# Decoder block on one core: cross-attention scores made once and the probabilities turned, and more PSUM banks for the last group's experts

## The chip, the cores and the metric

The kernel runs on one core of a Trainium2 chip. The metric is device time in microseconds (us) of one execution; lower is better. The engines named below are TensorE (PE; PEld is its weight load), VectorE (DVE), ScalarE (ACT), GpSimd (POOL) and SyncE (SP).

## The reference

For 128 sequences of 64 tokens with 128 features, one pre-norm decoder block: agent attention, causal cross-attention to a context, and a mixture of experts. Cut to what the change touches:

```python
# cross-attention: 16 heads of 8 features
Q = split_heads(query @ Wq.T); K = split_heads(key @ Wk.T); V = split_heads(value @ Wv.T)
scores = einsum('bhqd,bhkd->bhqk', Q, K) / sqrt(8)
attn = softmax(scores + causal, axis=-1)          # over the keys k
out = merge_heads(einsum('bhqk,bhkd->bhqd', attn, V)) @ Wo.T
# experts: 16 routed (2 chosen per token) and 2 shared ones, computed for all tokens
h = silu(x @ We1 + be1) * (x @ We3 + be3)
y = sum over the chosen experts of weight * (h @ We2 + be2), plus the shared experts
```

The block is `x += attn(ln(x)); x += xattn(ln(x), ctx); x += ffn(ln(x))`.

## The kernel before

The 128 sequences are worked in 8 groups of 16 (1024 tokens, 8 tiles of 128). The program runs 9 **periods** `(e, g)`: the experts of group `e` are interleaved with the attention of the following group `g`. Period 0 is `(None, 0)`, attention alone; period 8 is `(7, None)`, experts alone. Each engine has its own instruction stream, written out by hand as a function `both(e, g)`; the engines meet through semaphores, and each runs its stream in order.

The experts are 18 **units** per group. For unit `k` TensorE makes H1 and H3 (three 128x512 products each, `up`), spreads the expert weight (C, `weight`) and runs the down-projection of unit `k-1` (`down_to`); ScalarE applies Silu to H1 (`silu`); VectorE multiplies by H3 and by C (`hidden`, two instructions), which frees the H3 and C banks and makes hT.

PSUM has 8 banks. H1, H3, C and the output Y have one bank each; attention has a ring of four. The list `attention_tiles` writes out in which order attention's tiles take the ring, and a tile may be written once its predecessor four places earlier has been read. `wait_free` is this wait, placed ahead of a tile's first matmul; `read` says which semaphore frees each tile.

Cross-attention of a group is done in four parts `u` of 256 tokens, four tiles of 128x512 each (4 heads by 64 keys by 2 token tiles). Before the change it goes through the scores twice:

1. Within units 12 to 15, `scores(g, u)` makes the four tiles S with tokens on the partitions, and VectorE's `maxima` takes the row maxima. Nothing else is read from S.
2. After unit 15, `split_shifts` splits the maxima into three bf16 parts, `turn_shifts` turns them, ScalarE moves them into `shiftT`.
3. After unit 16, for each `u`, `scores_T(g, u)` makes the four tiles ST with the keys on the partitions: first `pickT`/`shiftT` matmuls put mask and minus maxima into the bank, then 32 small matmuls add K times Q. ScalarE's `exp_x` takes Exp from PSUM into `PT`, `values` multiplies `PT` by V into O, VectorE's `normalise_O` divides by the sums, `turn_O` and `project` make Yx, and `add_x` adds it to the residual. Parts of the next group's front (`front_xn`, `front_M`) lie between.

Then come unit 17, the gate of the experts of group `g` and the next period. The first half of the gate (`apply_e(g, 0)`, `gate_shift`, `gate_groups`) is worked here, the second at the start of the next period; the next period's unit 1 needs it, through `turn_3(e, 1)` on TensorE.

On ScalarE a change between Silu and Exp puts an ACT_TABLE_LOAD into the stream.

"Stage" in the text below is the stretch from the start of unit 12 (in period 0: of the first scores) to the end of the last projection or down-projection of a period.

Of the kernel before, what the change touches and what calls it, by code (L numbers as in the profile page):

```python
# [6 lines left out]
def decoder_block(nc, x, ctx_in, Wqkv, Wo_a, bo, Wq, Wk, Wv, Wo_x, gate_w, gate_b,  # L7
# [53 lines left out]
    MOMENTS = [(), (0, 1, 2), (3, 4, 5), (6, 7)]  # L61

    def attention_tiles(e, g):
# [18 lines left out]
        add(g, *[f"S_{k}" for k in range(XS)], "mT")  # L82
        for u in range(UX):
            add(g, *[f"ST_{XQ * u + q}" for q in range(XQ)])
            if u:
                add(g, f"OT_{u - 1}")
                add(n, *[f"M_{k}" for k in MOMENTS[u]])
            else:
                add(n, "xnT1_0", "xnT1_1")
            add(g, f"O_{u}")  # L90
            if u:
                add(g, f"Yx_{u - 1}")
        add(g, "xnT3_0", "gate_0", f"OT_{UX - 1}", f"Yx_{UX - 1}")
# [8 lines left out]
    place = {}  # L102
    for ring, (tiles, n) in RINGS.items():
        for at, tile in enumerate(tiles):
            place[tile] = (ring, at % n, at // n, tiles[at - n] if at >= n else None)

    with ExitStack() as ctx:
# [3 lines left out]
        def sem(name):  # L111
# [153 lines left out]
        read["mT"] = (mT_ready, 1, 0)  # L265
        for n in range(XS):
            read |= {f"S_{n}": (mx_ready, XS, n), f"ST_{n}": (ex_ready, XS, n)}
# [15 lines left out]
        issued = {ring: 0 for ring in RINGS}  # L283

        def wait_free(pe, g, name):

            ring, k, use, before = place[name, g]
            assert RINGS[ring][0][issued[ring]] == (name, g), (name, g, RINGS[ring][0][issued[ring]])
            issued[ring] += 1
# [55 lines left out]
        def _(pool):  # L345
# [22 lines left out]
            nc.gpsimd.memset(mparts[:], 0.0)  # L368
            nc.gpsimd.memset(shiftT[:], 0.0)
            nc.gpsimd.memset(combs[:], 0.0)  # L370
            nc.gpsimd.memset(onehot3[:], 0.0)
            step(nc.gpsimd.memset(pickT[:], 0.0))
# [16 lines left out]
            step(nc.gpsimd.affine_select(out=shiftT[0:S].rearrange("p (b q) -> p b q", q=S),  # L389
                                         in_=shiftT[0:S].rearrange("p (b q) -> p b q", q=S), compare_op=ALU.is_ge,  # L390
                                         fill=MASKED, base=0, pattern=[[0, GB], [1, S]], channel_multiplier=-1))
            step(nc.gpsimd.affine_select(out=pickT[0:S], in_=pickT[0:S], compare_op=ALU.not_equal, fill=1.0, base=0,
                                         pattern=[[0, XH // 2], [0, 2], [-1, S]], channel_multiplier=1))
            for k in range(3):
                step(nc.gpsimd.affine_select(out=pickT[S:P], in_=pickT[S:P], compare_op=ALU.not_equal, fill=1.0,
                                             base=-XH * k, pattern=[[-2, XH // 2], [-1, 2], [0, S]],
                                             channel_multiplier=1))
# [57 lines left out]
        def _(pe):  # L455
# [179 lines left out]
            def turn_shifts(g):  # L635

                wait_free(pe, g, "mT")
                pe.wait_ge(mp_ready, g + 1)
                for t in range(T):
                    last = turn_over(ps(g, "mT")[:].bitcast(bf16)[S:P, P * t:P * t + P], mparts[:, t, :], identb[:])  # L640
                last.then_inc(fulled(g, "mT"), 1)

            def scores_T(g, u):

                names = [f"ST_{XQ * u + q}" for q in range(XQ)]
                if u == 0:
                    pe.wait_ge(mT_ready, g + 1)
                for q, name in enumerate(names):
                    wait_free(pe, g, name)
                    for j in range(2):  # L650
                        mm(ps(g, name)[:, 256 * j:256 * j + 256], pickT[:, 2 * q + j, :, :],  # L651
                           shiftT[:, 256 * u:256 * u + 256], start=(j == 0), stop=False, skip_group_check=True)
                for j in range(2):
                    for k in range(4):
                        b = 4 * u + k
                        for q, name in enumerate(names):
                            rr = slice(32 * q, 32 * q + 32)
                            c0 = 256 * j + S * k
# [148 lines left out]
            def both(e, g):  # L807
# [63 lines left out]
                for u in range(UX):  # L871
                    unit(e, 12 + u)
                    if g is not None:
                        scores(g, u)
# [616 lines left out]
```

## Time and profile before

| what | value |
|---|---|
| median of 3 runs | 1214.93 us (1214.87 to 1220.33) |
| the profiled execution | 1225.85 us, of which the span is 1224.1 us |
| mean granted TensorE clock (profiled) | 0.914 of full speed |
| TensorE busy / weight loads busy | 85% / 70% of the span |
| VectorE / ScalarE / GpSimd busy | 56% / 41% / 10% of the span |
| chain that ended last, by engine | PE 61%, DVE 21%, ACT 11% |

A granted clock of 1.0 is 2.4 GHz, 0.5 is 1.2 GHz; a stretch in between was partly at either. Busy shares are means over stages with different limits, so the text goes by stage.

### The profile page before, as it was taken

The page shows a single profiled execution, that of the slowest core. Times are in us where ns is not written, and L with a number is a line of the kernel's source. Part 1 is how long each engine was busy: PE and PEld are TensorE (multiplying, and loading weights), DVE is VectorE, ACT ScalarE, POOL GpSimd, SP SyncE. Part 2 cuts the span into 40 slices and gives each one's busy share as a digit, 9 for nine tenths or more (in the row PEclk, how much of TensorE's full clock was granted, in tenths as well). Part 3 has the DMA queues.
Part 4 walks back from the last instruction along what each step waited for, and adds up shares of the span by engine and source line. Part 5 has one row for each costly group of instructions (what it writes and reads, how often), then busy time and mean ns, then how long its engine had stood idle before and what let it go on. Part 6 is the DMA issues. An engine that isn't in the chain of part 4 may idle for free.

```text
span 1224.1 us, 26890 instructions
## 1 busy us (share of the span) xinstructions
PE 1034.5 (85%) x11548; PEld 852.1 (70%) x11629; DVE 687.6 (56%) x1985; ACT 496.5 (41%) x836; POOL 120.3 (10%) x125
## 2 busy tenths in 40 slices
PE   6767988989799887989789887988889897997687
PEld 5653877678676676768676776867776686766576
DVE  2554167662686447672676437782676527861564
ACT  4341344424534354433534354434544344332232
POOL 8100010100201011000201011000201001000100
PEclk9776689978999998999999998999999998996789
DMA  6100001000100001000100001000010000000000
GB/s 173 35 1 1 2 2 35 10 2 2 44 1 10 2 11 35 10 2 2 44 1 10 2 10 36 10 1 2 13 32 10 2 2 9 1 10 2 9 1 18
DMA packets 28409, 18.54 MB, mean 15 GB/s; under 512 B 7394, under 2 KB 26883, under 8 KB 28291
## 3 DMA queue, kind: packets, MB, share of 16 engines
q1 hardware_dynamic: 26402, 12.35, 3.8%
q0 software_dynamic: 1280, 4.20, 1.1%
q8 instruction: 92, 1.51, 0.5%
q10 hardware_dynamic: 608, 0.27, 0.1%
q14 instruction: 27, 0.21, 0.1%
HBM read 12.62 MB, written 4.19 MB: 14 GB/s over the span
## 4 chain that ended last, share of the span: by engine, by line
PE 61%; DVE 21%; ACT 11%; issue 4%; POOL 2%; POOLq 0%; DVEq 0%
PE banks L533 8%; PE banks L720 6%; PE banks L676 6%; PE banks L659 6%; PE banks L522 4%; PE banks L523 3%; PE banks L524 3%; ACT PXUT L997 3%; PE banks L651 3%; ACT KQ L962 3%; PE banks L771 2%; PE banks L629 2%; DVE sil L1264 2%; DVE mx L1316 2%; PE banks L490 2%
## 5 line engine op out<-in xcount | busy, mean ns | idle before, releaser
L941 ACT ACTIVATE sil<-banks,b 128x512 f32<-128x512 f32 x144 | 99.7, 693 | 213.2 <-PE banks L524 211.1
L1264 DVE SCALAR_TENSOR_TENSOR sil<-banks,b,sil 128x512 f32<-128x512 f32 x128 | 95.7, 748 | 142.0 <-ACT sil L941 125.7
L533 PE MATMUL banks<-w,hT 128*128 128x128 f32 x1152 | 158.2, 282 | 15.0 <-DVE hT L1271 8.6
L533 PEld LDWEIGHTS banks<-w,hT 128*128 128x128 f32 x1152 | 157.9, 200 | 14.3 <-DVE hT L1271 10.4
L1333 DVE RECIPROCAL rx<-banks 128x32 f32<-128x32 f32 x32 | 11.4, 358 | 237.1 <-PE banks L676 237.1
L997 ACT ACTIVATE PXUT<-banks 128x512 f32<-128x512 f32 x128 | 66.1, 602 | 154.0 <-PE banks L659 154.0
L1316 DVE TENSOR_REDUCE mx<-banks 128x8 f32<-128x512 f32 x128 | 79.4, 683 | 26.3 <-PE banks L629 26.3
L522 PE MATMUL banks<-xnT3l,w1h 128*128 128x512 f32 x144 | 75.5, 524 | 18.6 <-ACT sil L941 18.6
L1271 DVE TENSOR_TENSOR hT<-sil,banks 128x512 f32<-128x512 f32 x128 | 87.9, 687 | 4.4
L720 PE MATMUL banks<-pooled,A 128*128 128x128 f32 x512 | 77.2, 319 | 4.6 <-DVE pooled L1353 1.9
L676 PE MATMUL banks<-Vx,PXUT 128*64 128x18 f32 x2048 | 74.7, 223 | 7.4 <-ACT PXUT L997 7.4
L676 PEld LDWEIGHTS banks<-Vx,PXUT 128*64 128x64 f32 x2048 | 71.7, 154 | 12.6 <-ACT PXUT L997 9.3
L720 PEld LDWEIGHTS banks<-pooled,A 128*128 128x128 f32 x512 | 73.5, 231 | 9.5 <-issue 7.2
L490 PE MATMUL banks<-ident,xn 128*128 128x128 f32 x192 | 34.0, 325 | 47.0 <-DVE xn L1173 31.7
L659 PEld LDWEIGHTS banks<-KQ 32*128 32x128 f32 x2048 | 68.2, 208 | 7.9 <-issue 7.9
L659 PE MATMUL banks<-KQ 32*128 32x64 f32 x2048 | 72.8, 296 | 0.0
L934 ACT COPY KQ<-banks 128x256 f32<-128x256 f32 (+1 forms) x64 | 31.3, 489 | 96.8 <-PE banks L490 77.6
L522 PE MATMUL banks<-xnT3l,w3h 128*128 128x512 f32 x144 | 62.2, 432 | 7.2 <-DVE sil L1264 7.1
L934 ACT COPY M<-banks 128x512 f32<-128x512 f32 x80 | 46.9, 586 | 51.5 <-PE banks L720 30.6
L411 POOL TENSOR_TENSOR norm_a<-norm_a,mhalf 128x8 f32<-128x8 f32 x16 | 26.5, 1655 | 388.8 <-DVE norm_a L1142 388.8
L417 POOL TENSOR_TENSOR norm_e<-norm_e,mhalf 128x4 f32<-128x4 f32 x16 | 16.3, 1018 | 469.6 <-DVE norm_e L1142 469.6
L490 PEld LDWEIGHTS banks<-ident,xn 128*128 128x128 f32 x192 | 26.3, 167 | 51.2 <-DVE xn L1173 33.8
(204 smaller groups left out, 1979.5 us busy)
## 6 DMA issues: line engine op xcount, KB each, us to landing
xin<-in_x SPq DMA_DIRECT2D x8, 512.0 KB, 4.5
cin<-in_ctx SPq DMA_DIRECT2D x8, 512.0 KB, 5.7
out_x<-xr POOLq DMA_DIRECT2D x16, 256.0 KB, 2.8
KQ<-in_L_attn_Wqkv SPq DMA_DIRECT2D x3, 512.0 KB, 5.5
KQ<-in_L_ffn_We SPq DMA_DIRECT2D x2, 512.0 KB, 4.4
KQ<-in_L_attn_Wo SPq DMA_DIRECT2D x1, 512.0 KB, 8.2
w<-in_L_ffn_We SPq DMA_DIRECT2D x1, 512.0 KB
KQ<-in_L_ffn_ws SPq DMA_DIRECT2D x2, 64.0 KB, 4.4
```

What stands on the lines that cost most here:

```text
L490: last = turn_over(ps(g, name)[:, P * t:P * t + P], src[:, 4 * n + t, :], ident[:])
L522: mm(ps(e, name)[:], wh[:, 2 * p:2 * p + 2, :], xl, start=True, stop=False)
L533: mm(ps(e, name)[:, P * t:P * t + P], hT[:, k % 2, P * t:P * t + P], w2[:, pair[k], :], start=(n == 0 and t == 0), stop=False, skip_group_ ...
L659: last = mm(ps(g, name)[:, c0:c0 + S], Kx[rr, j, b, :], Qx[rr, S * b:S * b + S], start=False, stop=True, skip_group_check=True, tile_posit ...
L676: last = mm(ps(g, name)[64 * r:64 * r + 64, o0:o0 + w], PT[:, XQ * (u % 2) + j // 2, c0:c0 + S], Vx[:, 4 * u + k, j, :], start=True, stop= ...
L720: last = mm(ps(g, f"M_{n}")[:, P * k:P * k + P], A[:, 4 * (n % 4) + k, :], pooled[:], start=True, stop=True)
L934: cp(dst, ps(g, name)[:] if src is None else src).then_inc(ready, 1)
L941: nc.scalar.activation(sil[:, k % 2, :], ps(e, f"H1_{k}")[:], ACT.Silu, bias=b1[:, pair[k]:pair[k] + 1]).then_inc(sil_ready, 1)
L997: nc.scalar.activation(PT[:, k % (2 * XQ), :], ps(g, f"ST_{k}")[:], ACT.Exp).then_inc(ex_ready, 1)
L1264: V.scalar_tensor_tensor(sil[:, k % 2, :], ps(e, f"H3_{k}")[:], b3[:, p:p + 1], sil[:, k % 2, :], ALU.add, ALU.mult).then_inc(hid_ready, 1)
L1271: V.tensor_tensor(hT[:, k % 2, :], sil[:, k % 2, :], ps(e, f"C_{k}")[:], ALU.mult).then_inc(hT_ready, 1)
L1316: V.tensor_reduce(mx[:, 2 * u:2 * u + 2, 4 * q:4 * q + 4], sv, AX, ALU.max, negate=True).then_inc(mx_ready, 1)
```

## The change

The second set of scores, the split and turned maxima and all tiles and constants that they need are gone. S is now read twice by VectorE: `shifted` takes the row maximum of each tile and subtracts it, into an SBUF buffer `pr`; ScalarE takes Exp of `pr` in place; TensorE turns the four 128x128 blocks of each tile (`turn_probs_x`, tiles P in PSUM, named PT_k); ScalarE copies them into `PT` (`PT_moved`). `values` and what follows is as before. `PT` has four slots in place of eight.

The work is laid out in six steps, one for each of the units 12 to 17: in step `s`, TensorE turns part `s-1`, makes the scores of part `s`, runs unit `12+s`, turns O of part `s-2`, makes the values of part `s-1` and projects part `s-2`. The next group's `front_xn` goes to step 4 and all of `front_M` to step 5. VectorE's `norm_a` and `apply_a` of the next group move into steps 2 and 3.

In the last period the one-bank rings of H1, H3 and C take turns with three of attention's banks: odd places of the last group's tiles use banks 0, 1 and 2 of the ring; what attention tiles are left there use bank 3. From its unit 2 on, the last group's Silu also waits for hT of two units before.

```diff
@@ attention_tiles
-        add(g, *[f"S_{k}" for k in range(XS)], "mT")
-        for u in range(UX):
-            add(g, *[f"ST_{XQ * u + q}" for q in range(XQ)])
...
+        for step in range(UX + 2):
+            if 1 <= step <= UX:
+                add(g, *[f"PT_{XQ * (step - 1) + q}" for q in range(XQ)])
+            if step < UX:
+                add(g, *[f"S_{XQ * step + q}" for q in range(XQ)])
+            if step >= 2:
+                add(g, f"OT_{step - 2}")
+            if 1 <= step <= UX:
+                add(g, f"O_{step - 1}")
+            if step == UX:
                 add(n, "xnT1_0", "xnT1_1")
...
+            if step >= 2:
+                add(g, f"Yx_{step - 2}")
@@ places
+    LAST = GROUPS - 1
+    ALSO = {"h1": 0, "h3": 1, "c": 2}
...
+            if ring == "att" and (name, i) in attention_tiles(LAST, None):
+                slot = ("att", 3)
+            elif ring in ALSO and i == LAST and at % 2:
+                slot = ("att", ALSO[ring])
@@ TensorE
-            def scores_T(g, u):
...
+            def turn_probs_x(g, u):
+
+                for q in range(XQ):
+                    name = f"PT_{XQ * u + q}"
                     wait_free(pe, g, name)
...
+                    pe.wait_ge(pr_ready, XS * g + XQ * u + q + 1)
+                    for t in range(2):
+                        for j in range(2):
+                            src = pr[:, q, 256 * t + P * j:256 * t + P * j + P]
+                            c0 = 256 * j + P * t
+                            last = turn_over(ps(g, name)[:, c0:c0 + P], src, ident[:])
+                    last.then_inc(fulled(g, name), 1)
...
+                for step in range(UX + 2):
+                    if g is not None and 1 <= step <= UX:
+                        turn_probs_x(g, step - 1)
+                    if g is not None and step < UX:
+                        scores(g, step)
+                    unit(e, 12 + step)
...
+                    if step >= 2:
+                        turn_O(g, step - 2)
+                    if 1 <= step <= UX:
+                        values(g, step - 1)
...
+                    if step >= 2:
+                        project(g, step - 2)
@@ ScalarE
+                if e == LAST and k >= 2:
+                    act.wait_ge(hT_ready, UNITS * e + k - 1)
...
-                wait_full(act, g, f"ST_{k}")
-                nc.scalar.activation(PT[:, k % (2 * XQ), :], ps(g, f"ST_{k}")[:], ACT.Exp).then_inc(ex_ready, 1)
+                act.wait_ge(dx_ready, XS * g + k + 1)
+                p = pr[:, k % XQ, :]
+                nc.scalar.activation(p, p, ACT.Exp).then_inc(pr_ready, 1)
...
+                for step in range(UX + 2):
+                    if g is not None and 1 <= step <= UX:
+                        PT_moved(g, step - 1)
+                    if g is not None and step < UX:
+                        exp_x(g, XQ * step)
+                        exp_x(g, XQ * step + 1)
+                    if g is not None and 2 <= step < UX:
+                        O_moved(g, step - 2)
+                    if g is not None and step < UX:
+                        exp_x(g, XQ * step + 2)
+                        exp_x(g, XQ * step + 3)
+                    silu(e, 12 + step)
@@ VectorE
+            def shifted(g, u):
 
                 for q in range(XQ):
                     k = XQ * u + q
                     wait_full(dve, g, f"S_{k}")
...
+                    link(V.tensor_reduce(mx[:, q], sv, AX, ALU.max))
+                    if u:
+                        wait_full(dve, g, f"PT_{k - XQ}")
+                    V.tensor_tensor(pr[:, q, :].rearrange("p (h s) -> p h s", s=S), sv,
+                                    mx[:, q].unsqueeze(2).to_broadcast([P, HALF, S]), ALU.subtract).then_inc(dx_ready, 1)
...
+                for step in range(UX + 2):
+                    if g is not None and step < UX:
+                        shifted(g, step)
...
+                    hidden(e, 12 + step)
...
+                    if step == 2 and nxt is not None:
+                        dve.wait_ge(x_loaded, 16 * nxt + 16)
+                        norm_a(xin)
+                    if step == 3 and nxt is not None:
+                        apply_a(xin, 2 * nxt + 1)
+                    if 1 <= step <= UX:
+                        normalise_O(g, step - 1)
...
+                    if step >= 2:
+                        add_x(g, step - 2)
```

How the order of the streams moves is seen at three places. The first is TensorE in period 1, around the work of the second part of cross-attention. In the rows L651 and L659 are the scores made again, L685 is `turn_O`, L720 `front_M`, L676 `values`, L694 `project`. Before:

```order
L651 MATMUL banks0<-shiftT,pickT 128x256 [waits On_ready]
L651 MATMUL banks0<-shiftT,pickT 128x256
L659 MATMUL banks0<-KQ 128x64
...
L685 MATMUL banks0<-ident,KQ 128x128 [waits ex_ready]
L685 MATMUL banks0<-ident,KQ 128x128
L720 MATMUL banks1<-pooled,A1 128x128 [waits ex_ready,pooled_ready]
...
L676 MATMUL banks0<-Vx,PXUT 64x18 [waits ex_ready,OT_ready]
L676 MATMUL banks0<-Vx,PXUT 64x18 x31
L694 MATMUL banks1<-xwT,KQ 128x128 [waits OT_ready,M_ready]
```

Now, from `values` of part 1 in step 2 to the first rows of the scores of part 3 in step 3 (L653 is `values`, L672 `project`, L639 the turned probabilities, L615 the mask rows of the scores):

```order
L653 MATMUL banks1<-Vx,PXUT 64x18 [waits pT_ready,dx_ready]
L653 MATMUL banks1<-Vx,PXUT 64x18 x31
L672 MATMUL banks1<-xwT,KQ 128x128 [waits OT_ready,dx_ready]
L672 MATMUL banks1<-xwT,KQ 128x128
L639 MATMUL banks0<-ident,PXUT 128x128 [waits pr_ready,dx_ready]
...
L639 MATMUL banks0<-ident,PXUT 128x128 [waits pr_ready,OT_ready]
...
L639 MATMUL banks1<-ident,PXUT 128x128 [waits pr_ready,On_ready]
...
L639 MATMUL banks1<-ident,PXUT 128x128 [waits pr_ready,xattn_added]
L639 MATMUL banks1<-ident,PXUT 128x128 x3
L615 MATMUL banks0<-maskb,pick 64x512 [waits pT_ready] x2
L615 MATMUL banks1<-maskb,pick 64x512 [waits pT_ready] x2
```

The turned probabilities of one part now stand between two sets of scores, and their last two tiles wait in the ring for `normalise_O` (On_ready) and `add_x` (xattn_added) of earlier parts; the next scores wait for the copies of these tiles (pT_ready).

The second place is ScalarE in period 1. Before, from unit 12 on (L941 Silu, L997 Exp, L934 copies):

```order
L941 ACTIVATE sil<-banks2,b1 128x512 [waits h10_full] x5
L934 COPY shiftT<-banks1 64x1024 [waits att2_full]
L997 ACT_TABLE_LOAD
L997 ACTIVATE PXUT<-banks1 128x512 [waits att3_full]
L997 ACTIVATE PXUT<-banks0 128x512 [waits att0_full]
L997 ACTIVATE PXUT<-banks0 128x512 [waits att1_full]
L997 ACTIVATE PXUT<-banks1 128x512 [waits att2_full]
```

Now, steps 1 and 2 (L909 are copies, of P into PT where PXUT is written; L978 is Exp, L918 Silu):

```order
L909 COPY PXUT<-banks0 128x512 [waits att0_full]
...
L978 ACT_TABLE_LOAD
L978 ACTIVATE PXUT<-PXUT 128x512 [waits dx_ready] x4
L918 ACT_TABLE_LOAD
L918 ACTIVATE sil<-banks2,b1 128x512 [waits h10_full]
L909 COPY PXUT<-banks0 128x512 [waits att1_full,att0_full]
L909 COPY PXUT<-banks1 128x512 [waits att2_full]
L909 COPY PXUT<-banks1 128x512 [waits att3_full]
L909 COPY PXUT<-banks0 128x512 [waits att0_full]
L978 ACT_TABLE_LOAD
L978 ACTIVATE PXUT<-PXUT 128x512 [waits dx_ready] x2
```

Five Silus stood together and now each stands behind four Exps, with two table loads a step; the copies of the turned tiles stand behind the Silu.

The third place is VectorE in period 1, step 2 (L1303 and L1306 are `shifted`, L1251 and L1258 `hidden`, L1314 and L1315 `normalise_O`, L1321 `add_x`):

```order
L1306 TENSOR_TENSOR PXUT<-banks0,mx 128x512 [waits att0_full,vec_step]
L1251 SCALAR_TENSOR_TENSOR sil<-banks2,b3,sil 128x512 [waits sil_ready,h30_full]
L1258 TENSOR_TENSOR hT<-sil,banks3 128x512 [waits c0_full,hid_ready]
L1134 BN_STATS stats_a<-xin 128x6 [waits x_loaded]
L1134 BN_STATS stats_a<-xin 128x6 x7
...
L1129 SCALAR_TENSOR_TENSOR norm_a6<-norm_a3,norm_a5 128x8 [waits vec_step]
L1314 RECIPROCAL rx<-banks1 128x32 [waits att2_full]
L1315 TENSOR_TENSOR KQ<-banks1,rx 128x256 [waits vec_step]
L1321 TENSOR_TENSOR xr1<-xr1,banks1 128x256 [waits att3_full]
```

`normalise_O` and `add_x`, which free the banks of the first place, now stand behind `hidden`, and that waits for the Silu of the second place.

## Rows read from the trace of the kernel before

**Rows 1.** Stages by windows (length, busy us and counts per engine, PEclk): periods 0, 7; 1 to 6.

```profile
96.00:169.50 73.50, 60.10 (x854) 46.51 (x854) 22.92 (x64) 18.99 (x37) 2.28 (x2) 0.72 0.01 2
...
1080.90:1153.30 72.40, 61.43 (x883) 51.04 (x887) 27.70 (x63) 21.55 (x36) 2.30 (x2) 0.79 0.01 2
...
sum 411.41, PE 366.75 PEld 306.74 DVE 186.56 ACT 165.45 POOL 23.63; mean PE 61.13 PEld 51.12 DVE 31.09 ACT 27.58 POOL 3.94
```

**Rows 2.** Groups by line, TensorE (busy us, mean ns, idle before and its releasers).

```profile
L490 PE MATMUL banks<-ident,xn 128*128 128x128 f32 x192 | 34.0, 325 | 47.0 <-DVE xn L1173 31.7 <-DVE xn L1165 10.0 <-ACT PXUT L997 5.3
...
L659 PE MATMUL banks<-KQ 32*128 32x64 f32 x2048 | 72.8, 296 | 0.0
```

**Rows 3.** Timeline of TensorE, period 1, unit 14 and after it (start, length, count).

```profile
247.42 0.50 PE L522 MATMUL banks<-xnT3l,w1h 128*128 128x512 f32 x1
...
250.14 0.64 PE L621 MATMUL banks<-maskb,pick 32*64 32x512 bf16 x16
...
251.57 0.50 PE L522 MATMUL banks<-xnT3l,w1h 128*128 128x512 f32 x1
...
290.48 2.92 PE L720 MATMUL banks<-pooled,A 128*128 128x128 f32 x24
293.33 2.05 PE L676 MATMUL banks<-Vx,PXUT 128*64 128x18 f32 x64
...
304.68 0.60 PE L490 MATMUL banks<-ident,xn 128*128 128x128 f32 x4
```

**Rows 4.** Timeline of VectorE, periods 0 and 1.

```profile
59.69 0.69 DVE L1291 TENSOR_REDUCE m<-banks 128x64 f32<-128x512 f32 x1
60.41 0.69 DVE L1292 TENSOR_TENSOR PXUT<-banks,m 128x512 f32<-128x512 f32 x1
...
89.61 1.64 DVE L1147 BATCH_NORM_STATS2 stats_a<-xin 128x6 f32<-128x128 f32 x8
...
116.20 2.13 DVE L1165 TENSOR_SCALAR xn<-xin,norm_a 128x128 f32<-128x128 f32 x8
130.38 0.36 DVE L1333 RECIPROCAL rx<-banks 128x32 f32<-128x32 f32 x1 [12.04 <-PE banks L676]
130.77 0.42 DVE L1334 TENSOR_TENSOR KQ<-banks,rx 128x256 f32<-128x256 f32 x1
...
212.25 0.75 DVE L1264 SCALAR_TENSOR_TENSOR sil<-banks,b,sil 128x512 f32<-128x512 f32 x1 [2.62 <-ACT sil L941]
213.03 0.69 DVE L1271 TENSOR_TENSOR hT<-sil,banks 128x512 f32<-128x512 f32 x1
```

**Rows 5.** Timeline of ScalarE, periods 1 and 2.

```profile
239.04 1.08 ACT L934 COPY ctxT<-banks 128x512 f32<-128x512 f32 x2
...
326.26 0.69 ACT L941 ACTIVATE sil<-banks,b 128x512 f32<-128x512 f32 x1 [0.25 <-PE banks L524]
326.96 1.28 ACT L1009 ACT_TABLE_LOAD   x1
328.26 0.63 ACT L1009 ACTIVATE e<-e 128x512 f32<-128x512 f32 x1
```

**Rows 6.** Timeline of VectorE at the start of period 2.

```profile
315.83 0.42 DVE L1340 TENSOR_TENSOR xr<-xr,banks 128x256 f32<-128x256 f32 x1
...
317.59 0.21 DVE L1224 TENSOR_REDUCE g<-gate 128x4 f32<-128x64 f32 x1
```

**Rows 7.** Stretches of the last period, by windows.

```profile
1164.20:1168.00 3.80, 3.80 (x14) 3.04 (x14) 0.00 (x0) 2.38 (x5) 1.28 (x1) 0.50 0.02 4
...
1171.00:1189.00 18.00, 16.51 (x93) 12.35 (x94) 13.73 (x43) 5.68 (x8) 0.00 (x0) 1.00 0.01 1
```

**Rows 8.** Timeline of GpSimd and VectorE in the setup.

```profile
22.31 1.16 POOL L389 TENSOR_SCALAR_AFFINE_SELECT shiftT<-shiftT 64x1024 bf16<-64x1024 bf16 x1 [0.52 <-POOL pick L387]
...
24.91 3.78 POOL L395 TENSOR_SCALAR_AFFINE_SELECT pickT<-pickT 64x1024 bf16<-64x1024 bf16 x3
...
31.03 0.17 DVE L1122 TENSOR_REDUCE plane<-planes 128x4 f32<-128x16 f32 x1 [19.01 <-POOL spread L402]
```

More of the change, by code:

```diff
@@ L81, in attention_tiles @@
         add(n, "ctxT_0", "ctxT_1")
-        add(g, *[f"S_{k}" for k in range(XS)], "mT")
-        for u in range(UX):
-            add(g, *[f"ST_{XQ * u + q}" for q in range(XQ)])
[L85 to L88, printed above, removed]
-                add(n, "xnT1_0", "xnT1_1")
[L90 to L93, printed above, removed]
+        for step in range(UX + 2):
[8 more added lines that the diff above has]
+            if step == UX:
+                add(n, "xnT1_0", "xnT1_1")
+                add(g, "xnT3_0")
+            if step > UX:
+                add(g, "gate_0")
+                add(n, *[f"M_{k}" for k in range(8)])
+            if step >= 2:
+                add(g, f"Yx_{step - 2}")
         return tiles
@@ L101, in decoder_block @@
              "y": ([(f"Y_{c}", e) for e in range(GROUPS) for c in range(CHUNKS)], 1)}
-    place = {}
+    LAST = GROUPS - 1
+    ALSO = {"h1": 0, "h3": 1, "c": 2}
+    home, turns, place = {}, {}, {}
     for ring, (tiles, n) in RINGS.items():
-        for at, tile in enumerate(tiles):
-            place[tile] = (ring, at % n, at // n, tiles[at - n] if at >= n else None)
+        for at, (name, i) in enumerate(tiles):
+            slot = (ring, at % n)
+            if ring == "att" and (name, i) in attention_tiles(LAST, None):
+                slot = ("att", 3)
+            elif ring in ALSO and i == LAST and at % 2:
+                slot = ("att", ALSO[ring])
+            line = turns.setdefault(slot, [])
+            place[name, i] = (*slot, len(line), line[-1] if line else None)
+            line.append((name, i))
     with ExitStack() as ctx:
@@ L281, in ps @@
             return bank[place[name, g][0]][place[name, g][1]]
-        issued = {ring: 0 for ring in RINGS}
+        issued = {slot: 0 for slot in turns}
         def wait_free(pe, g, name):
             ring, k, use, before = place[name, g]
-            assert RINGS[ring][0][issued[ring]] == (name, g), (name, g, RINGS[ring][0][issued[ring]])
-            issued[ring] += 1
+            assert turns[ring, k][issued[ring, k]] == (name, g), (name, g)
+            issued[ring, k] += 1
             if before is not None:
@@ L388, in _ @@
                                                  base=32 * a, pattern=[[-1, S]], channel_multiplier=1))
[L389 to L397, printed above, removed]
             for k in range(3):
@@ L683, in turn_O @@
                 wait_free(pe, g, f"OT_{u}")
+                pe.wait_ge(On_ready, UX * g + u + 1)
                 for t in range(2):
@@ L1463, in both @@
                     gate_groups(g, 0)
-                    add_x(g, UX - 1)
-                    norm_e(g, 1)
                     gate_best(g, 0, 0)
```

169 lines of the change are left out of this document (45 added, 124 removed).

## Prediction

> **What bounds the kernel now.** I read first the page's shares (TensorE busy 85%, VectorE 56%, ScalarE 41%), then the stages by windows, then the timelines of three engines. Cross-attention with units 12 to 17 is one stage a period [rows 1]: in periods 1 to 6 six stages take 411.4 us, 68.6 each, with TensorE busy 366.75/411.41 = 89%, VectorE 45%, ScalarE 40%. So TensorE bounds this stage, and the scores made again are on its path: their small matmuls alone are 72.8 us over 8 groups [rows 2]. Periods 0 and 7 have stages of 73.5 and 72.4 us, with a mean granted clock of 0.72 and 0.79. The chain of waits says the same (61% on TensorE). The reader is to see that no engine is full after the change either; what counts is therefore whether the new waits, in order, are longer than the work they replace.
>
> **TensorE's work in the changed stage.** At a granted clock of 1.0, a unit takes 250.14 - 247.42 = 2.72, one part's scores 251.57 - 250.14 = 1.43, four transposes 0.60, one part's values 2.05, and the eight M tiles (64 records at 24 in 2.92) 7.8 [rows 3]. Four scores, six units, sixteen turned tiles, four values, M and ten short pieces (turned O, projections, turned x, gate, last down-projection), which I take at 0.6 each, make 5.7 + 16.3 + 9.6 + 8.2 + 7.8 + 6.0 = 53.6 us. If only this counted, a stage would lose 15 us. It is not what I expect to count.
>
> **The round trip of one part.** Time zero is when the four S tiles of a part are full. The added operations have near relatives in the trace: for the reduction and subtraction of a 128x512 tile from PSUM I take the soften pair, for Exp in place the agent's Exp.
>
> - VectorE: the subtraction starts 0.72 after the reduction and lasts 0.69, so four tiles take 4 x 1.41 = 5.6 [rows 4].
> - ScalarE: Exp of the last tile 0.63, to 6.3. Behind it in order stand a table load and the unit's Silu: 1.28 to 7.5, 0.69 to 8.2 [rows 5]. H1 has long been full, so the load is not hidden, unlike the one to Exp, which runs while ScalarE waits for VectorE.
> - VectorE next has `hidden` of this unit, which needs that Silu: it idles from 5.6, then 213.03 + 0.69 - 212.25 = 1.47, to 9.7. Behind it stands `normalise_O` of the part before, 0.36 + 0.42 with hand-over 0.8, to 10.5, then `add_x` 0.4, to 10.9 [rows 4].
> - TensorE: the last turned tiles may be written only when these two have freed their banks. Then four transposes 0.6, copy to PT 0.6, and the rest of the next scores 1.4, because all four of its banks were held by turned tiles: 2.6 together. Behind these waits stand, in order, the next unit and all that follows.
>
> Step by step at full clock: step 0 has no O yet, but the four copies stand behind the Silu, so 8.2 + 4 x 0.49 [rows 5] + 1.4 = 11.6. Step 1: 10.5 + 2.6 = 13.1. Step 2 has `norm_a` between `hidden` and `normalise_O`: eight statistics 1.64 [rows 4] and seven small ones 0.9 (1.76 of [rows 6] less `add_x` 0.42 and two statistics 0.4), so 10.9 + 2.6 + 2.6 = 16.1. Step 3 has `apply_a`, 2.13: 13.0, and 0.6 for the last transposes, 13.6. From there TensorE runs on: two units, values, M and ten pieces, 5.4 + 2.05 + 7.8 + 6.0 = 21.3. Ahead of step 0, the first scores wait for the copies of ctxT (to 240.12, against 239.15 for unit 12 now) and take 1.4: 2.4. The sum is 2.4 + 11.6 + 13.1 + 16.1 + 13.6 + 21.3 = 78.1 us against 68.6: 9.5 more in each of six periods. The TensorE work within the steps (unit, O, values, projection: at most 6 us from zero) ends long before 10.5, so the pauses are 4 to 6 us.
>
> **The clock.** After TensorE's pause of 9.5 us in the last period the granted clock is 0.50, that is 1.2 GHz, over the next 3.8 us of full work [rows 7]; in the stage of period 0, where TensorE and VectorE take turns, it is 0.72 on average [rows 1]. With pauses of 4 to 6 us in each step I expect the lower level behind them. If the whole of a round trip's TensorE part ran at half speed, 1.4 would be added in step 0, 2.0 in each of steps 1 and 2, 0.6 in step 3 and 2.7 in unit 16: 8.7. If none did, nothing. I take 6, nearer to the upper end, by period 0: a stage of 84.1, 15.5 more than now, 93 us over six periods.
>
> **The other terms.**
> - Period 7 has no next group: without `norm_a`, `apply_a`, M and the turned x, 78.1 - 2.6 - 2.1 - 7.8 - 1.2 = 64.4, with the clock 70.4, against 72.4: -2 (-8 to +1).
> - Period 0 has no units, so no Silu, load or `hidden`: the steps are 6.3 + 2.0 + 1.4 = 9.7, 9.8, 12.0 and 9.5, then 14.7, ahead 2.3: 58, with the clock 64, against 73.5: -9 (-15 to -7).
> - The gate's first half now comes with `add_x` and `norm_e` of the last part ahead of `result`, where VectorE waits anyway. Between them and `gate_best` it did 317.59 - 315.83 = 1.76 [rows 6] on the way to the turned xn3, for which TensorE waits 31.7 us in all [rows 2]. Eight periods: -14 (0 to -14).
> - The last group's extra banks: TensorE idles 18.00 - 16.51 = 1.5 us over six units there [rows 7] and the rest runs at its own pace, so -1 (0 to -1.5). The added wait for hT of two units before lies behind a down-projection that needs the same hT: nothing, and 0.7 a unit, one Silu, if that cover were gone.
> - Setup: GpSimd's constants of the second scores go (22.31 to 28.69 and three memsets earlier), and VectorE's first statistics wait 19 us for the end of GpSimd's list [rows 8]. I take -6, up to 6.4; nothing if TensorE's own setup ends later than that list.
> - ScalarE's 16 copies and 6 more table loads a period, and VectorE's 16 subtractions, cost only where the round trip counts them; VectorE comes to 31 + 11 of 84 us busy. No DMA is added and no queue of SP changes.
>
> Sum: 93 - 2 - 9 - 14 - 1 - 6 = +61. Against the profiled execution, 1225.85, that is 1287; the median of the runs is 0.9% under it, so **1275 us**, 5% slower. Half a per cent (6 us) is about what a measurement of this kernel can tell from no change.
>
> The Trainium skill, "ScalarE: Activation LUTs", What ACT_TABLE_LOAD costs, puts a switch at 1283 ns for the load plus some 1380 ns of drain. Here Silu ends at 326.95, the load starts at 326.96 and Exp follows at 328.26 [rows 5]: the load agrees, the drain is not there. With the drain four exposed switches a stage would add 4 x 1.38 x 7 = 39 us to the sum.
>
> **Rivals.**
> - *TensorE-bound after all (not slower).* The units fill the waits, a stage takes 53.6 + 2.4 = 56 and period 7 about 43: 6 x -12.6, -29, -25 (period 0) and -21 for starts, last group and setup, 1225.85 - 151 or 1065 in median. For it: no engine is full. Against it: the ring wait of the last turned tiles and the Silu's place are in the order, not in a budget. It decides where the four steps together fall below 50 us (52 if the clock stays high) instead of 54.4: then the stage costs 74 to 76 and the other gains pay for it. The Trainium skill, "Perfetto Trace Analysis", Optimization Strategy, advises interleaving regimes with different bounds, which is this rival; it also takes a repeated gap on the engine that should be full as a sign that the next tile finds no PSUM, which is the forecast.
> - *The same round trip at full clock.* 6 x 9.5 - 8 - 15 - 14 - 1 - 6 = +13: 1228. For it: TensorE has 2.7 us of dense work in each step. Against: the pauses.
> - *Half clock throughout*: 6 x 18.2 + 1 - 7 - 14 - 1 - 6 = +82, 1296.
> - *A drain at each switch*, by the Trainium skill's figure: about 1314. The trace speaks against it.
> - *The gain is swallowed and nothing is left*: the step pairs run 0.08 shorter a tile (an overlap that successive VectorE instructions show), 0.3 a step, 9 us in all, and the clock stays high: 1219.
>
> **How the numbers follow.** Round trip with a clock between (1250 to 1300): 0.58. Half clock throughout or the drain (1290 to 1320): 0.12. Full clock (1222 to 1240): 0.13. Nothing left (1209 to 1221): 0.07. TensorE-bound, fully or in part (below 1209): 0.10. The range of 8 in 10 runs from 1221 to 1308; the likeliest case alone has 1250 to 1300. Faster 0.10, same 0.07, slower 0.83.
>
> **What would show it.** In the changed profile: VectorE idle of about 2.6 us ahead of `hidden` (released by Silu) in steps 0 to 3; the third and fourth turned tiles of a part released by `normalise_O` and `add_x`; steps of 11 to 12, 13, 16 us at the least; granted clock well below 0.9 in the stages; TensorE busy below 80%; the first M tiles some 6 us earlier. The forecast is wrong if the last turned tiles are released by Exp, if the load ahead of Silu overlaps the last Exp's wait, or if steps come at TensorE's own 8 to 9 us.

## The result, and the profile after

The changed kernel takes **1278.74 us** in the median (1273.31 to 1279.36, 4 runs), the kernel before 1217.63 in the same series: 4.9% slower, ratio 1.0489 (95% interval 1.0441 to 1.0537). The forecast was 1275 us, slower.

The profiled execution of after is its fastest, 1273.31 us (span 1271.6, mean granted clock 0.907); that of before, 1225.85, lies 0.7% above its median. On the profiles the difference is therefore 47.5 us, on the medians 61. The page of after (shares of the span, then the chain that ended last):

```profile
PE 1008.0 (79%) x9691; PEld 811.7 (64%) x9773; DVE 769.5 (61%) x2081; ACT 623.0 (49%) x998; POOL 112.5 (9%) x117
...
PE 43%; DVE 34%; ACT 13%; issue 7%; POOL 2%; DVEq 0%; POOLq 0%
```

TensorE was 61% of that chain and is 43%; VectorE rose from 21% to 34%. No engine is full. The stages by windows, as in [rows 1]: period 0 and period 7, and the six mixed ones (the second row stands for them, all lie within 83.24 to 83.60).

```profile
79.89:140.50 60.61, 49.27 (x622) 40.70 (x622) 34.20 (x86) 27.23 (x51) 3.91 (x3) 0.77 0.01 1
...
365.32:448.80 83.48, 62.48 (x722) 49.26 (x727) 44.26 (x107) 44.28 (x67) 3.95 (x3) 0.86 0.00 1
...
1132.47:1201.10 68.63, 53.19 (x648) 40.59 (x655) 38.77 (x83) 38.05 (x56) 2.31 (x2) 0.88 0.01 2
```
```profile
sum 500.69, PE 374.44 PEld 295.43 DVE 265.56 ACT 265.73 POOL 23.70; mean PE 62.41 PEld 49.24 DVE 44.26 ACT 44.29 POOL 3.95
```

Six stages went from 411.41 to 500.69: TensorE's busy time in them rose by 8 us only, its idle time from 45 to 126. That is the loss. By stretches:

| stretch | before | after | difference | forecast |
|---|---|---|---|---|
| start to the first scores of period 0 | 96.0 | 79.89 | -16.1 | -6 (setup) |
| stage of period 0 | 73.50 | 60.61 | -12.9 | -9 |
| six mixed stages | 411.41 | 500.69 | +89.3 | +93 |
| stage of period 7 | 72.40 | 68.63 | -3.8 | -2 |
| last period, to the end of the span | 70.8 | 70.5 | -0.3 | -1 and its start |
| starts and middles of periods 1 to 7 (the rest) | | | -8.7 | -14, with the start of the last |

Two long waits, by line (busy us, mean ns, idle before and its releasers); the first is VectorE's, the second TensorE's:

```profile
L1251 DVE SCALAR_TENSOR_TENSOR sil<-banks,b,sil 128x512 f32<-128x512 f32 x128 | 96.0, 750 | 189.4 <-ACT sil L918 173.4
L639 PE MATMUL banks<-ident,PXUT 128*128 128x128 f32 x512 | 88.9, 325 | 122.1 <-DVE KQ L1315 105.9
```

The turned probabilities (L639) wait 105.9 us for `normalise_O` (L1315), and `hidden` (L1251) waits for the Silu. These are the two waits that the forecast named. The 173.4 us are over all 18 units: 101.9 of them are left in run 1 below, where only the four steps change, so the steps hold some 71, about 2.6 in each of 28. One round trip shows how they hang together; first VectorE in period 2 (the first reduction of steps 0 to 3, and all of step 2):

```profile
367.70 0.69 DVE L1303 TENSOR_REDUCE mx<-banks 128x8 f32<-128x512 f32 x1 [4.51 <-PE banks L623]
...
380.55 0.69 DVE L1303 TENSOR_REDUCE mx<-banks 128x8 f32<-128x512 f32 x1 [3.23 <-PE banks L623]
...
395.11 0.69 DVE L1303 TENSOR_REDUCE mx<-banks 128x8 f32<-128x512 f32 x1 [4.21 <-PE banks L623]
...
399.81 0.69 DVE L1306 TENSOR_TENSOR PXUT<-banks,mx 128x512 f32<-128x512 f32 x1
403.26 0.75 DVE L1251 SCALAR_TENSOR_TENSOR sil<-banks,b,sil 128x512 f32<-128x512 f32 x1 [2.76 <-ACT sil L918]
404.05 0.69 DVE L1258 TENSOR_TENSOR hT<-sil,banks 128x512 f32<-128x512 f32 x1
404.65 1.64 DVE L1134 BATCH_NORM_STATS2 stats_a<-xin 128x6 f32<-128x128 f32 x8
...
407.52 0.42 DVE L1315 TENSOR_TENSOR KQ<-banks,rx 128x256 f32<-128x256 f32 x1
407.86 0.41 DVE L1321 TENSOR_TENSOR xr<-xr,banks 128x256 f32<-128x256 f32 x1
...
413.15 0.69 DVE L1303 TENSOR_REDUCE mx<-banks 128x8 f32<-128x512 f32 x1 [4.35 <-PE banks L623]
```

The subtractions end at 400.50, `hidden` starts at 403.26 and `normalise_O` ends at 407.94, behind the statistics. On ScalarE at the same time stand the last Exp, the load, the Silu, and the copies of the turned tiles:

```profile
400.53 0.63 ACT L978 ACTIVATE PXUT<-PXUT 128x512 f32<-128x512 f32 x1 [0.69 <-DVE PXUT L1306]
401.18 1.28 ACT L918 ACT_TABLE_LOAD   x1
402.48 0.69 ACT L918 ACTIVATE sil<-banks,b 128x512 f32<-128x512 f32 x1
403.06 1.06 ACT L909 COPY PXUT<-banks 128x512 f32<-128x512 f32 x2
409.15 0.58 ACT L909 COPY PXUT<-banks 128x512 f32<-128x512 f32 x1 [5.03 <-PE banks L639]
```

And TensorE, which has turned two tiles by 401.75 and may write the other two at 408.00:

```profile
400.71 1.04 PE L639 MATMUL banks<-ident,PXUT 128*128 128x128 f32 x8
408.00 1.97 PE L639 MATMUL banks<-ident,PXUT 128*128 128x128 f32 x8 [6.25 <-DVE KQ L1315]
409.90 1.81 PE L615 MATMUL banks<-maskb,pick 32*64 32x512 bf16 x16
411.09 2.01 PE L623 MATMUL banks<-KQ 32*64 32x256 f32 x32
```

After its pause of 6.25 us, eight transposes take 1.97 in place of 1.04 and the scores 3.2 in place of 1.43 [rows 3]: the lower of the clock's two levels.

### The profile page after: what moved, and what is told of

Its sections match the earlier page's. It is cut to its first block, busy times and chain, and to the rows that moved or that the text cites. A ratio compares the mean times of both kernels' runs of the same rounds, so it can differ in the third digit from the quotient of the medians.

```text
span 1271.6 us, 23681 instructions
## 1 busy us (share of the span) xinstructions
PE 1008.0 (79%) x9691; PEld 811.7 (64%) x9773; DVE 769.5 (61%) x2081; ACT 623.0 (49%) x998; POOL 112.5 (9%) x117
## 3 DMA queue, kind: packets, MB, share of 16 engines
q8 instruction: 78, 1.28, 0.4%
## 4 chain that ended last, share of the span: by engine, by line
PE 43%; DVE 34%; ACT 13%; issue 7%; POOL 2%; DVEq 0%; POOLq 0%
DVE mx L1303 6%; PE banks L527 5%; PE banks L698 5%; DVE sil L1251 4%; PE banks L623 3%; PE banks L639 3%; DVE PXUT L1306 3%; PE banks L516 3%; PE banks L615 3%; ACT sil L918 3%; DVE hT L1258 3%; PE banks L517 3%; PE banks L518 3%; ACT KQ L939 3%; PE banks L749 2%
## 5 line engine op out<-in xcount | busy, mean ns | idle before, releaser
L1251 DVE SCALAR_TENSOR_TENSOR sil<-banks,b,sil 128x512 f32<-128x512 f32 x128 | 96.0, 750 | 189.4 <-ACT sil L918 173.4
L639 PE MATMUL banks<-ident,PXUT 128*128 128x128 f32 x512 | 88.9, 325 | 122.1 <-DVE KQ L1315 105.9
L1303 DVE TENSOR_REDUCE mx<-banks 128x8 f32<-128x512 f32 x128 | 87.5, 683 | 132.3 <-PE banks L623 132.3
L909 ACT COPY PXUT<-banks 128x512 f32<-128x512 f32 x192 | 104.3, 592 | 121.1 <-PE banks L639 83.0
L918 ACT ACTIVATE sil<-banks,b 128x512 f32<-128x512 f32 x144 | 99.8, 693 | 114.6 <-PE banks L518 111.9
L639 PEld LDWEIGHTS banks<-ident,PXUT 128*128 128x128 f32 x512 | 70.0, 167 | 134.1 <-DVE KQ L1315 110.9
L978 ACT ACTIVATE PXUT<-PXUT 128x512 f32<-128x512 f32 x128 | 80.7, 630 | 147.9 <-DVE PXUT L1306 147.9
L1306 DVE TENSOR_TENSOR PXUT<-banks,mx 128x512 f32<-128x512 f32 x128 | 88.5, 692 | 4.4
L1258 DVE TENSOR_TENSOR hT<-sil,banks 128x512 f32<-128x512 f32 x128 | 87.9, 687 | 4.4
L909 ACT COPY KQ<-banks 128x256 f32<-128x256 f32 (+1 forms) x64 | 30.5, 477 | 89.3 <-PE banks L484 48.3
L653 PE MATMUL banks<-Vx,PXUT 128*64 128x18 f32 x2048 | 68.6, 215 | 3.7 <-DVE PXUT L1306 3.3
L653 PEld LDWEIGHTS banks<-Vx,PXUT 128*64 128x64 f32 x2048 | 65.4, 143 | 9.3 <-DVE PXUT L1306 5.7
L615 PE MATMUL banks<-maskb,pick 32*64 32x512 bf16 x512 | 55.2, 546 | 16.5 <-ACT PXUT L909 14.7
L909 ACT COPY M<-banks 128x512 f32<-128x512 f32 x80 | 46.8, 586 | 43.3 <-PE banks L698 23.7
L698 PE MATMUL banks<-pooled,A 128*128 128x128 f32 x512 | 59.3, 277 | 6.5 <-DVE pooled L1334 6.5
L698 PEld LDWEIGHTS banks<-pooled,A 128*128 128x128 f32 x512 | 57.8, 192 | 7.5 <-DVE pooled L1334 7.5
L517 PE MATMUL banks<-xnT3h,w1l 128*128 128x512 f32 x144 | 60.8, 422 | 0.0
```

Source lines behind the costliest of these rows:

```text
L517: mm(ps(e, name)[:], wl[:, 2 * p:2 * p + 2, :], xh, start=False, stop=False)
L639: last = turn_over(ps(g, name)[:, c0:c0 + P], src, ident[:])
L653: last = mm(ps(g, name)[64 * r:64 * r + 64, o0:o0 + w], PT[:, j // 2, c0:c0 + S], Vx[:, 4 * u + k, j, :], start=True, stop=True)
L698: last = mm(ps(g, f"M_{n}")[:, P * k:P * k + P], A[:, 4 * (n % 4) + k, :], pooled[:], start=True, stop=True)
L909: cp(dst, ps(g, name)[:] if src is None else src).then_inc(ready, 1)
L918: nc.scalar.activation(sil[:, k % 2, :], ps(e, f"H1_{k}")[:], ACT.Silu, bias=b1[:, pair[k]:pair[k] + 1]).then_inc(sil_ready, 1)
```

## The experiments

Every kernel below is the changed kernel with one edit; times are medians of 4 executions, beside the 1216.4 to 1216.6 us of the kernel before, timed along with them.

**1. The Silu ahead of the Exps**

```diff
@@ ScalarE
                         PT_moved(g, step - 1)
+                    if step < UX:
+                        silu(e, 12 + step)
                     if g is not None and step < UX:
                         exp_x(g, XQ * step)
...
                         exp_x(g, XQ * step + 3)
-                    silu(e, 12 + step)
+                    if step >= UX:
+                        silu(e, 12 + step)
```

> Changed kernel, but in steps 0 to 3 ScalarE makes the unit's Silu ahead of the part's Exps in place of behind them. Same instructions on every engine. Ordered round trip (my theory): `hidden` no longer waits for the Silu (2.76 us in each of steps 1 to 3 in the changed profile), and in step 0 the copies of the turned tiles stand behind the last Exp alone (2.6 earlier), so 10.9 us less a stage in periods 1 to 7, 76 in all: about 1203 us, 1190 to 1220. Rival, the sheer amount of work added to VectorE and ScalarE: nothing moves, 1279. Rival, the half clock is the cost and not the waits: under 20 us, 1260 to 1279.

Measured: 1184.22 us, ratio 0.972 (0.968 to 0.976), 94.5 less than the changed kernel and 6 below the range that was expected. VectorE's wait for the Silu is gone from these steps; the load to Exp now runs while VectorE makes the first reductions and subtractions (from 370.30), and the Exps follow it (ScalarE, period 2, step 1):

```profile
371.19 0.69 ACT L918 ACTIVATE sil<-banks,b 128x512 f32<-128x512 f32 x1 [1.17 <-PE banks L518]
371.89 1.28 ACT L978 ACT_TABLE_LOAD   x1
373.19 1.84 ACT L978 ACTIVATE PXUT<-PXUT 128x512 f32<-128x512 f32 x3
```

The window of that stage has 69.51 us at a clock of 0.95, where the changed kernel has 83.48 at 0.86: 14.0 less, 3 more than the 10.9 that the expectation took for the waits alone; TensorE's pauses at the ring are shorter (3.5 us at most, 6.4 before) and the clock is higher. The rival "amount of work" falls.

**2. The banks freed ahead of `hidden`**

```diff
@@ VectorE
+                    if g is not None and 1 <= step < UX:
+                        normalise_O(g, step - 1)
+                    if g is not None and 2 <= step < UX:
+                        add_x(g, step - 2)
                     hidden(e, 12 + step)
...
-                    if 1 <= step <= UX:
+                    if step == UX:
                         normalise_O(g, step - 1)
...
+                    if step >= UX:
+                        add_x(g, step - 2)
                     if step >= 2:
-                        add_x(g, step - 2)
```

> Changed kernel, but in steps 1 to 3 VectorE makes `normalise_O` and `add_x` ahead of `hidden` (and of the next group's statistics) in place of behind them. Same instructions. Ordered round trip: the last turned tiles find their banks free right behind the subtractions; the copies then stand behind the Silu alone. By the changed profile of period 2 that is 1.65 us less in step 1, 5.4 in step 2, 6 in step 3, so 13 a stage in six periods, 8 in period 7 and 4 in period 0 (the statistics come later there): about 1189 us, 1175 to 1225. Rival, amount of work: 1279. Rival, half clock alone: 1260 to 1279.

Measured: 1200.85 us, ratio 0.987 (0.983 to 0.991), 77.9 less; the stage in period 2 takes 72.04, 11.4 less. TensorE's wait for `normalise_O` does not appear any more (the changed kernel's 105.9 us):

```profile
L639 PE MATMUL banks<-ident,PXUT 128*128 128x128 f32 x512 | 72.1, 290 | 16.2 <-ACT PXUT L978 16.2
```

The copies still stand behind the Silu, as expected. So the ring wait is a cause of its own, and the Silu's place is another.

**3. Both**

> Both reorderings together, same instructions as the changed kernel. Ordered round trip: behind the subtractions (5.6 us from full S tiles) come `normalise_O` 6.4 and `add_x` 6.8, the last Exp ends at 6.3, so the turned tiles end at 8.1, their copies at 8.7, the next scores at 9.8; TensorE's own work in a step is 9.6. Four steps take about 38 us in place of 59.5: 21 less in six periods, 17 in period 7, 4 in period 0, about 1130 us, 1110 to 1160, and so faster than the kernel before (1215). Rival, amount of work: 1279. Rival, half clock alone: 1260 to 1279.

Measured: **1138.28 us**, ratio 0.936 (0.933 to 0.939): 6.4% faster than the kernel before, 140 us less than the changed kernel with the same instructions. TensorE in period 2, from step 2 into step 3, and the windows of steps 0 (with the first scores) to 3 and of the whole stage:

```profile
377.48 2.05 PE L653 MATMUL banks<-Vx,PXUT 128*64 128x18 f32 x64
379.46 0.71 PE L672 MATMUL banks<-xwT,KQ 128*128 128x128 f32 x4
380.09 1.97 PE L639 MATMUL banks<-ident,PXUT 128*128 128x128 f32 x16
381.99 1.58 PE L615 MATMUL banks<-maskb,pick 32*64 32x512 bf16 x16
383.20 1.23 PE L623 MATMUL banks<-KQ 32*64 32x256 f32 x32
```
```profile
353.13:364.97 11.84, 9.76 (x128) 5.91 (x128) 6.59 (x10) 8.39 (x13) 0.00 (x0) 1.00 0.00 1
364.97:374.54 9.57, 9.25 (x147) 6.88 (x144) 7.28 (x12) 7.60 (x11) 0.00 (x0) 1.00 0.01 3
374.54:384.37 9.83, 9.60 (x154) 7.49 (x150) 9.48 (x24) 7.88 (x12) 0.00 (x0) 1.00 0.01 2
384.37:393.91 9.54, 8.80 (x106) 8.07 (x102) 9.26 (x24) 6.28 (x10) 1.66 (x1) 0.82 0.01 2
353.13:415.10 61.97, 57.32 (x720) 46.90 (x726) 43.38 (x106) 43.95 (x67) 3.97 (x3) 0.97 0.01 2
```

Sixteen transposes run on without a wait. Steps 1 to 3 take 9.5 to 9.8 us with TensorE busy for 8.8 to 9.6 of them, and the stage 61.97 in place of 83.48. The two gains together (140) are less than their sum (172): TensorE now fills the steps, and VectorE almost as much (9.48 us of step 2, 9.26 of step 3, where TensorE waits 0.67 us for a subtraction).

**4 and 5. TensorE kept busy in the pauses**

```diff
+            def fill(e, u):
+                if e is None or u == 0:
+                    return
+                pe.wait_ge(sil_ready, UNITS * e + 12 + u + 1)
+                for _ in range((0, 4, 11, 10)[u]):
+                    mm(ps(e, f"H1_{13 + u}")[:], w1h[:, 0:2, :], xnT3l[:, 0:CH], start=True, stop=True)
...
                 for q in range(XQ):
+                    if q == (3 if u == 1 else 2):
+                        fill(e, u)
```

Run 4 had (5, 11, 11, 10), with tile 3 held back in part 0 and tile 2 in the others; run 5 is the one printed.

> Changed kernel with 5, 11, 11 and 10 extra 128x512 products ahead of the turned tiles that wait for `normalise_O` (steps 1 to 4), written into the free H1 bank and overwritten by the next unit; the waits are as before. Theory that pauses of TensorE cost the clock: the steps 1 to 3 and the tail exceed their sum at full clock by 4.1 us a stage; if the clock stays up, 3 to 4 us come back in each of seven stages: about 1255 us, 1248 to 1265. If the clock falls for another reason, or the extra products run past the end of the pauses: 1275 to 1295.

Measured: 1277.40 us, the same as the changed kernel and not the 1255 that was expected. Its trace shows why this says little. In parts 0 and 1 the extra work held back tiles whose banks were free, and in period 2, from unit to unit, these steps took 0.7 and 0.9 us more; parts 2 and 3 took 1.8 and 0.8 less, but in four of the six mixed stages part 2 took only 0.4 to 0.7 less. Over the six stages the four steps came to the same (357.2 us against 357.6). Unit 16 and what follows up to unit 17 gained 1.1 in each, and the stretch from unit 2 to unit 12 lost 1.6 in each (last section).

> Changed kernel with 4, 11 and 10 extra 128x512 products in the three pauses that end with `normalise_O` (parts 1, 2, 3), where the earlier version also held back tiles that had no such wait. In the earlier run the two steps whose pause alone was filled came out 1.8 and 0.8 us shorter. Pauses cost the clock: 1.5, 1.8 and 0.8 us less in each of seven stages, 28 in all at most, about 1255 us (1250 to 1265). The clock is not worth anything here, because it is lost again elsewhere: 1270 to 1280.

Measured: 1255.27 us, ratio 1.032 (1.028 to 1.035), 23.5 less than the changed kernel with 25 more products a stage. The wait for `normalise_O` stays, and in most stages the level behind it no longer falls (TensorE, steps 3 and 4 of period 2, and step 3 of period 3 in the last row; L635 are the extra products):

```profile
401.39 2.84 PE L635 MATMUL banks<-xnT3l,w1h 128*128 128x512 f32 x11 [1.57 <-ACT sil L928]
406.18 1.97 PE L649 MATMUL banks<-ident,PXUT 128*128 128x128 f32 x8 [1.95 <-DVE KQ L1325]
408.08 1.71 PE L615 MATMUL banks<-maskb,pick 32*64 32x512 bf16 x16
409.27 1.38 PE L623 MATMUL banks<-KQ 32*64 32x256 f32 x32
...
423.17 1.09 PE L649 MATMUL banks<-ident,PXUT 128*128 128x128 f32 x8 [1.76 <-DVE KQ L1325]
424.01 0.48 PE L516 MATMUL banks<-xnT3l,w1h 128*128 128x512 f32 x1
...
556.97 1.09 PE L649 MATMUL banks<-ident,PXUT 128*128 128x128 f32 x8 [1.96 <-DVE KQ L1325]
```

In part 3 the transposes behind the pause take 1.09. In part 2 of period 2 they still take 1.97, behind another pause of 1.95 after the extra products, and the scores 2.6 us (408.08 to 410.65) in place of 3.2; in the five other mixed stages the same pause (1.95 to 1.97) is followed by 1.09, so this pause alone does not decide the level. From unit 13 to unit 16 the three filled steps take 13.27, 16.24 and 13.42 us in those five, where the changed kernel takes 14.56, 18.03 and 14.20 in period 2. By the starts of the units the stages of periods 1 to 7 give back 30 us from unit 12 to unit 17, and 11 are lost again from unit 2 to unit 12 (last section); the profiles differ by 19.7, the medians by 23.5. So the clock is a cost of the pauses, and 23.5 us is what is left of it in the time.

**6. The removed constants put back**

The three memsets and five selections of `pickT`, `shiftT` and `mparts` stand in GpSimd's list again; nothing reads them.

> Changed kernel with GpSimd's constants of the second scores (three memsets, five selections) put back into the setup; nothing reads them. My prediction gave their removal 6 us; the trace after has VectorE's first statistics 9.2 us earlier. If GpSimd's list alone sets the start: 9 us slower than the changed kernel, 1288. If only 6 of it counts: 1285. If something else in the setup ends later: 1279.

Measured: 1288.64 us, ratio 1.059 (1.056 to 1.062), 9.9 slower. VectorE's first wait, in this kernel and in the changed one:

```profile
31.03 0.17 DVE L1124 TENSOR_REDUCE plane<-planes 128x4 f32<-128x16 f32 x1 [19.00 <-POOL spread L411]
```
```profile
21.86 0.17 DVE L1109 TENSOR_REDUCE plane<-planes 128x4 f32<-128x16 f32 x1 [10.38 <-POOL spread L396]
```

GpSimd's list alone sets the start: 9.2 us of it, 9.9 in the time.

**7. No table load between Exp and Silu**

```diff
-                nc.scalar.activation(sil[:, k % 2, :], ps(e, f"H1_{k}")[:], ACT.Silu,
+                nc.scalar.activation(sil[:, k % 2, :], ps(e, f"H1_{k}")[:], ACT.Exp if 12 <= k < 16 else ACT.Silu,
```

Exp stands in place of Silu in units 12 to 15: the kernel leaves out the Silu of these units.

> Changed kernel with Exp in place of Silu for the units 12 to 15, so that part of the experts' computation is another function; no table load stands between a part's Exps and the unit's activation in steps 0 to 3, all else in its order. Ordered round trip with a load of 1.28 us: 1.28 less in each of four steps of seven stages, 36 in all, about 1243 us, down to 1230 if the shorter pauses also cost less clock. A load with a drain behind it (2.66 together): 74 less, 1205. Loads hidden behind the wait for VectorE: 1279.

Measured: 1231.70 us, ratio 1.013 (1.009 to 1.016), 47.0 less. VectorE's wait ahead of `hidden` falls from 2.76 to 1.34:

```profile
374.04 0.75 DVE L1251 SCALAR_TENSOR_TENSOR sil<-banks,b,sil 128x512 f32<-128x512 f32 x1 [1.34 <-ACT sil L918]
```

1.42 less in each of 28 steps is 40 us. So the load lies on the path with its 1.28 and next to nothing behind it. The other 7 us are put down to the shorter pauses, as was expected; no run takes them apart.

**8. The last group on its own banks again**

`LAST`'s odd tiles go back to their rings, and the Silu's wait for hT is taken out with them.

> Changed kernel with the last group's experts back on one bank each of H1, H3 and C, attention's tiles on their ring of four, and no wait of Silu for hT. My prediction gave the banks 1 us, so 1280; the trace after shows the last period 0.5 us shorter than before, with a new wait of 1.17 us for ScalarE's copy of the turned xn3 at its start: 1278 to 1280 in time, unit 1 some 1.2 us earlier and units 2 to 11 about 0.7 us longer in the trace.

Measured: 1276.45 us, ratio 1.049 (1.045 to 1.052): no change that can be told, though 1.5 us below the range that was expected. The trace shows the start of the last period, here (first row) and in the changed kernel:

```profile
1215.72 0.63 PE L738 MATMUL banks<-identb,combs 128*128 128x128 bf16 x4
```
```profile
1213.23 0.61 PE L738 MATMUL banks<-identb,combs 128*128 128x128 bf16 x4 [1.17 <-ACT xnT3h L998]
```

With one bank left for attention's tiles the changed kernel waits 1.17 us for ScalarE's copy of the bank. Its unit 1 so starts 1.3 us later after unit 0 and takes 1.0 longer; its units 2 to 11 take 28.9 us, this kernel's 29.6. From the first product of the last period to the end of the span it takes 70.5 us (1201.11 to 1271.6), this kernel 68.8 (1204.97 to 1273.8).

## Why the prediction was right, point by point

- **The round trip** was right, place by place. By the first reductions of steps 0 to 3 and the start of unit 16 (427.23 on TensorE) the steps take 12.85, 14.56, 18.04 and 14.08; forecast at full clock were 11.6, 13.1, 16.1 and 13.6, ahead and tail 2.4 and 21.3 (measured 2.38 and 21.57). The sum is 83.48 against 84.1. What exceeds the full-clock sum is 5.4 us, against the 6 taken for the clock. Runs 1, 2 and 3 show the cause: the same instructions in another order take 94, 78 and 140 us less. Run 5 shows the full-clock sums of the filled steps: 13.27, 16.24 and 13.42.
- **The clock** was right in kind and about right in size: run 5 gives back 23.5 us without shortening the wait for `normalise_O`. In its stages, with three of the pauses filled, it is 4.7 to 5.0 us (five of the six mixed ones); step 0, which it leaves as it was, lies 1.25 above its full-clock sum. Together that is near the 6 that was taken; the sum of the rows has 5.4, since the tail at full clock was put some 0.8 too high (run 5 takes 20.45 for the 21.3). The reason given, pauses of 4 to 6 us in each step, fits steps 2 and 3 (6.2 and 5.9) and nearly step 1 (3.6), but not step 0: there TensorE works in pieces with waits of 0.4 to 1.8 us between them, and the scores behind them take 4.2 us in place of 1.43 (TensorE, period 2):

```profile
376.28 2.53 PE L615 MATMUL banks<-maskb,pick 32*64 32x512 bf16 x16 [1.76 <-ACT PXUT L909]
378.18 2.33 PE L623 MATMUL banks<-KQ 32*64 32x256 f32 x32
```
- **The rivals.** TensorE-bound after all (1065) is not what this order does, but run 3 is this rival with the order mended: from the first scores to unit 16 it takes 40.8 us, where the changed kernel takes 61.9 (365.32 to 427.23), and it beats both kernels. Its 1138 us lie above 1065: a mixed stage takes 61.97, not 56 (TensorE is busy for 57.3 of it, not 53.6), the stage of period 0 58.4, not 48.5, and that of period 7 50.9, not 43, which is 54 of the 73 us; the starts gain less too. The Trainium skill, "Perfetto Trace Analysis", Optimization Strategy, says that a repeated gap on the engine that should be full can mean too little PSUM for the next tile. By run 2 the trace agrees in that the tile found no free bank (105.9 us); but the banks were enough in number, and freeing them earlier took the wait away. The drain behind a load, which the Trainium skill gives in "ScalarE: Activation LUTs", What ACT_TABLE_LOAD costs, is not there: run 7 shortens the wait by 1.42 us, where load and drain would have given 2.66, an estimate by that page's figure.
- **Setup** was mis-sized: -6 forecast, -6.4 at most, and -9.2 to -9.9 measured (run 6). The working counted the selections of [rows 8] (6.4 us) as the upper bound and left out the memsets ahead of them, though it named them.
- **Period 0** came to -12.9 against -9, within its bounds of -15 to -7: first scores to last projection take 60.6 where 64 were expected. A further 6.1 us lie between the first M tiles and the first scores (54.4 before, 48.3 after), which no term held. In the seven other kernels with this setup and this order there, that stretch takes 49.9 to 53.3 at a granted clock of 0.86 to 0.81; it was 0.89 here and 0.79 in the profile of before. So 1.6 to 5.0 of the 6.1 belong to this one execution, and how much of the rest the change brings is not shown.
- **The starts** came to less than the -14. Where VectorE waits for `result`, as the step said, the gain is there: from `result` to the end of the turned rows' inputs 1.7 us less. But period 1 has no experts ahead of it, hence no `result` to wait for, and `add_x` with `norm_e` now stands in the way of the gate (unit 1 comes 12.3 us after unit 0, 10.9 before); and in the last period the gain goes into the wait of run 8. "VectorE waits anyway" held in six periods of eight.
- **The last group's banks** have the wrong sign in the trace (run 8: 1.7 us better without them), at a size that the time can't tell. The gain in units 2 to 11 is there (0.7 for the 1 that was forecast); the wait at the start of the period, which was not foreseen, outweighs it.
- **The sum**, +61, equals the difference of the medians, but the profiles differ by 47.5: the terms were set against an execution of before above its median, and the unforeseen 6 us and the larger gains of setup, period 0 and period 7 stand against smaller ones at the starts. The agreement to 0.3% is in part luck; the step that decides, +93 against +89.3, is not.

## What to carry to other kernels

Work that is saved on the fullest engine is worth nothing if the new order makes that engine wait: write out the round trip of one part, engine by engine, and look at what stands in order between the last input and the instruction that frees a bank. On an in-order engine, put what others wait for (here the freeing of banks, and the Silu that needs another table) ahead of what only fills the time; here two such moves turned 4.9% slower into 6.4% faster. A pause of the matmul engine can cost twice, for itself and for the slower clock behind it.

## What the hardware showed that was not expected

A pause is not always followed by the lower level. The same wait of 2.23 us in period 2, in the changed kernel and in run 5 (TensorE; the fourth product behind the wait):

```profile
325.27 0.63 PE L586 MATMUL banks<-ident,PXUT 128*128 128x128 f32 x4 [2.23 <-DVE PXUT L1288]
...
326.43 0.39 PE L516 MATMUL banks<-xnT3l,w3h 128*128 128x512 f32 x1
```
```profile
323.10 0.63 PE L586 MATMUL banks<-ident,PXUT 128*128 128x128 f32 x4 [2.23 <-DVE PXUT L1298]
...
324.29 0.63 PE L516 MATMUL banks<-xnT3l,w3h 128*128 128x512 f32 x1
```

From unit 2 to unit 12 (with the first scores), where the edits touch no instruction, this period so takes 53.5 us at a granted clock of 1.00 in the first and 55.0 at 0.97 in the second. Both values occur within one kernel too: in run 2 this stretch takes 53.5 us in periods 2 and 6 and 55.0 in periods 1, 3 and 4; in the kernel before, where the stretch has no scores, it takes 51.0 and 52.6 in turn. A kernel can thus lose 1.5 us a period in a stretch that nobody changed; what decides it is not settled here.
